# Row sums of an attention softmax: the inversion moved from VectorE's reciprocal to a power of minus one on GpSimd

## Chip, cores and metric

The kernel runs on one core of a Trainium2 chip. The metric is the device time of one execution in microseconds; lower is better. Below, PE is TensorE, DVE is VectorE, ACT is ScalarE, POOL is GpSimd and SP is SyncE, as in the profile.

## What is computed

Eight images of 256 channels and 32x32 points (1024 tokens) pass through three layers: a group norm with full softmax attention over 8 heads of 32 channels, a linear attention with rotary angles and a short convolution, and a feed-forward layer on a Haar transform. Only the first one's softmax is touched:

```python
weight = jnp.einsum('bct,bcs->bts', q * scale, k * scale)
weight = jax.nn.softmax(weight.astype(jnp.float32), axis=1)
a = jnp.einsum('bts,bcs->bct', weight, v)
```

The kernel keeps the axis s on the partitions and t, over which the softmax runs, along the free dimension, so that maximum and sum are taken within a partition.

## The kernel before

**Units and blocks.** One image has 64 units (`UNITS`): 2 groups of 4 heads (`NG`, `HG`), 8 blocks of 128 key positions (`NB`), and within a block the 4 heads of the group. Unit s makes one 128x1024 tile of scores: PE's `scores` (L653, two matmuls into one of two PSUM tiles ps_s), DVE's `maximum` (L1053, negmax), ACT's `exponentials` (L914), which writes probs and adds the rows up into `sums`. A PSUM tile comes free for the scores two units on when its exponential is done.

**Values.** When the 4 units of a block are through, its 128x4 sums are inverted, and the block's 128x128 values are multiplied by them (`v_scaled`, two buffers), which does the softmax's division on the smaller side. PE's `weigh_values` (L668, 16 matmuls) then adds probs times v_scaled into ps_o. Three steps on three engines, joined by semaphores: DVE's `invert_sums` (L1059) waits for probs_ready and raises rsums_ready; POOL's `scale_values` (L1330) waits for v_done, for pv_done (its buffer has been read), and for rsums_ready, and raises v_scaled_ready, for which `weigh_values` waits. There are 128 such blocks in all, 16 an image.

**Order.** Each engine runs its own instruction stream in order. The loops go over images in kinds (first, six steady, last, and an epilogue) and over the 64 units; behind a unit's own instruction stand the steps that tables such as `DVE_STEADY` or `POOL_STEADY` give to that slot. While image i is in its attention, the later layers of image i - 1 and the preparation of image i + 1 are spread over the same slots. In `DVE_STEADY`, `"invert"` has 16 slots (2, 5, 8, 12, ...), and in `POOL_STEADY`, `"scale"` has 16 (0, 5, 6, 12, 17, 17, 25, ...). Entries of one slot come in the order of the table.

**What else POOL does.** The square-root inverses of the norms (`rsqrt`: an addition L1361, ln_var, then a power with the exponent -0.5, L1364, ln_rs, with a wait of POOL on its own semaphore between), the convolution's products and sums (`lepe`: L1369, L1386, L1389), the mean of the keys (L1401, L1404, kmean), and the rotation of the queries (`turn_q`: L507, L511, L514). PE's denominators (L768) wait for kmean; PE's linear attention output (L781, "out") waits for the last L514 of its half of the heads, and DVE's L1199 follows it. PE's L741 projects queries and keys of the second layer, L749 transposes its keys. DVE's L1224 is the last addition of an image.

Of the kernel before, what the change touches and what calls it, by code (L numbers as in the profile page):

```python
# [13 lines left out]
P = 128  # L14
# [13 lines left out]

CONSTS = {}
_at = 0  # L30
for _name, _width in (("gn_mean", P), ("minus_half", 4), ("eps", 2), ("ident", P), ("head_mask", P),
                      ("head_mean", HG), ("pair_rows", P // 2), ("interp", NC * LL),
                      ("cos_tok", NB * D), ("sin_tok", NB * D),
                      ("cos_ch", L), ("sin_ch", L)):
    CONSTS[_name] = (_at, _at + _width)
    _at += _width
# [7 lines left out]
for _name, _width in (("bq", 2), ("bk", 2), ("bproj", 2), ("bqk", 4), ("lepe_w", 6), ("lepe_bias", 6),  # L44
# [19 lines left out]
    "copy": (36, 37), "pk0": (48, 56), "apply": (40, 43), "pq1": (12, 12), "pq0": (43, 44), "pk1": (20, 22),  # L64
}
DVE_FIRST = {
    "invert": (5, 9, 13, 17, 21, 25, 29, 33, 37, 41, 45, 49, 52, 57, 60), "w1": (25, 29), "pv0": (47, 62),
    "pk1": (21, 23), "pq1": (13, 13), "stats": (31, 32, 37, 38), "moments": (38,), "gn": (38,), "pq0": (45, 45),
    "pk0": (53, 57), "pv1": (2, 9),
}  # L70
# [18 lines left out]
DVE_STEADY = {  # L89
    "pv0": (47, 63), "norm1": (11, 14, 16, 16), "norm2": (42, 45, 46, 47), "pk1": (21, 21), "proj": (5, 7, 8, 9),  # L90
    "x1T": (10, 11, 12, 15), "kT": (24, 27, 31, 32), "kv": (30, 35),
    "invert": (2, 5, 8, 12, 16, 20, 25, 28, 32, 36, 41, 44, 48, 54, 56, 60), "denT": (33,),
# [21 lines left out]
    "qk": (18, 18, 21, 22, 24, 25, 28, 30),  # L114
}
DVE_LAST = {
# [126 lines left out]
def build(nc, x, wqkv_t, wproj_t, wqk, fc1_t, fc2_t, params, consts, out):  # L243
    with ExitStack() as ctx:
# [801 lines left out]
        def _(dve):  # L1046
# [6 lines left out]
                dve.tensor_reduce(negmax[:, s % 4:s % 4 + 1], ps_s[s % 2][:, :], AX_X, ALU.max, negate=True)\  # L1053
                   .then_inc(max_ready, 1)

            def invert_sums(i, g, j):
                n = NB * g + j
                dve.wait_ge(probs_ready, UNITS * i + HG * (n + 1))
                dve.reciprocal(rsums[:, j % 2, :], sums[:, j % 2, :]).then_inc(rsums_ready, 1)  # L1059

            def gn_statistics(b, n):

                c, half = n // 2, n % 2
# [190 lines left out]
            def step(kind, i, tile):  # L1254
                name, n = tile
                b = i - 1
                if name == "invert":
                    n = 2 * NB * i + n - (0 if kind == "first" else 1)
                    invert_sums(n // (2 * NB), n // NB % NG, n % NB)
                elif name == "w1":  # L1260
                    dve.wait_ge(made["w1"], n + 1)
                    dve.tensor_copy(w1[:, n * HALF:n * HALF + HALF], bank(tile)[:, :]).then_inc(weights_ready, 1)
                elif name == "norm1":
                    ln_normalise(b, n, x1_tokens(n), ln1_rsqrt, ln1_done)
                elif name == "norm2":
                    ln_normalise(b, n, t2_tokens(n), ln2_rsqrt, ln2_done)
                elif name == "add":
                    add_norm(dve, b, n)
                elif name == "lepe":
                    lepe_tail(b, n)  # L1270
                elif name == "late_turn":
                    turn_q(dve, b, n + 4)
                elif name == "stats":
                    gn_statistics(i + 1, n)
                elif name == "moments":
                    gn_moments(i + 1)
                elif name == "gn":
                    gn_group(i + 1)
                elif tile in SPLIT:
                    low_part(i, tile)  # L1280
                elif name in ("pv0", "pv1"):
                    values(i, tile)
                else:
                    post_tile(i, tile)
# [23 lines left out]
                        step(kind, i, tile)  # L1308

            def epilogue():  # L1310
                invert_sums(B - 1, NG - 1, NB - 1)
                for s in range(UNITS):
                    for tile in due("DVE", "epilogue", s):
                        step("epilogue", B, tile)
# [5 lines left out]
        def _(pool):  # L1320
            def scale_values(i, g, j):

                n = 2 * NB * i + NB * g + j
                pool.wait_ge(v_done, 4 * i + 2 * g + 2)
                if j >= 2 or not (isinstance(i, int) and i == 0 and g == 0):

                    pool.wait_ge(pv_done, 2 * (n - 1))
                pool.wait_ge(rsums_ready, n + 1)
                r = rsums[:, j % 2, :].rearrange("p (h o) -> p h o", o=1)
                pool.tensor_tensor(v_scaled[:, j % 2, :].rearrange("p (h d) -> p h d", h=HG),  # L1330
                                   v_tok[g][:, j, :].rearrange("p (h d) -> p h d", h=HG),
                                   r.to_broadcast([P, HG, D]), ALU.mult).then_inc(v_scaled_ready, 1)
# [125 lines left out]
def constants():  # L1458
# [15 lines left out]
    interp[np.arange(C), i0 + 1] = w  # L1474
    con["interp"][:] = interp.reshape(NC, P, LL).transpose(1, 0, 2).reshape(P, NC * LL)
    con["minus_half"][:] = -0.5
    con["eps"][:] = 1e-5
    inv_freq = (1.0 / np.float32(10000.0) ** (np.arange(0, D, 2, dtype=np.float32) / np.float32(D))).astype(np.float32)
    freqs = np.outer(np.arange(L, dtype=np.float32), inv_freq).astype(np.float32)
# [51 lines left out]
```

## Time and profile before

| | before |
|---|---|
| median of 3 runs | 1364.84 us (1364.63 to 1365.78) |
| the profiled execution | 1364.11 us |
| its span, first to last instruction | 1362.3 us |
| PE busy | 1235.3 us (91%) |
| DVE busy | 995.1 us (73%) |
| ACT busy | 879.5 us (65%) |
| POOL busy | 467.4 us (34%) |
| mean granted TensorE clock | 0.976 of 2.4 GHz |

Busy shares are averages over the whole span. A matmul counts as busy while it is in the pipeline, so 91% doesn't mean that PE is at its peak. The chain that ended last is found by going back from the last instruction, each time to what released it or to the instruction before it on its engine. "issue" is time in which the profile shows nothing that was waited for; where an instruction waits for two semaphores, the one that it names can be the wrong one.

### The profile page before, as it was taken

To read this page: it belongs to the slowest core of one execution; us is meant where nothing else is said; L and a number is where in the kernel's file an instruction comes from. 1 tells how busy PE (TensorE), PEld (TensorE's weight loads), DVE (VectorE), ACT (ScalarE), POOL (GpSimd) and SP (SyncE) were. 2 spreads that over 40 slices of the span, in tenths; PEclk is the share of its full clock that TensorE was granted. 3 is DMA by queue.
4 is the path that set the end of the run, shared out by engine and by line. 5 is a ranking of instruction groups with operands and counts; after the bars stand their busy time and mean duration, and the time that the engine had idled before them with its cause. 6 is when DMAs were issued, how large, how long until landed. Compare 5 with 4: busy or idle time off the path is not lost.

```text
span 1362.3 us, 22187 instructions
## 1 busy us (share of the span) xinstructions
PE 1235.3 (91%) x7972; PEld 644.5 (47%) x7972; DVE 995.1 (73%) x1609; ACT 879.5 (65%) x1457; POOL 467.4 (34%) x621
## 2 busy tenths in 40 slices
PE   6888899899998999899998999989998999979796
PEld 5544444544445454445444444454544444444373
DVE  3666687857889487866888578884879678884663
ACT  1666667675776668676775767766685767757422
POOL 2001017520285015630185203840166301850351
PEclk9998999999999999999999999999999999999897
DMA  8242415123442236223351234422262234300210
GB/s 275 58 108 45 106 40 134 34 63 101 110 112 47 52 109 139 48 63 93 92 116 27 66 117 101 105 57 58 88 140 48 62 93 110 80 15 0 80 33 31
DMA packets 51180, 110.84 MB, mean 81 GB/s; under 512 B 15456, under 2 KB 15840, under 8 KB 50816
## 3 DMA queue, kind: packets, MB, share of 16 engines
q1 hardware_dynamic: 48400, 100.39, 30.3%
q0 software_dynamic: 2480, 8.78, 2.3%
q8 instruction: 64, 1.05, 0.3%
q14 instruction: 44, 0.36, 0.1%
q10 hardware_dynamic: 192, 0.26, 0.1%
HBM read 21.81 MB, written 8.39 MB: 22 GB/s over the span
## 4 chain that ended last, share of the span: by engine, by line
PE 54%; DVE 29%; ACT 7%; issue 4%; POOL 2%; DMA 2%; SPq 1%; DVEq 0%; ACTq 0%; POOLq 0%
DVE negmax L1053 15%; PE ps_s L653 13%; PE ps_o L668 7%; PE work L741 6%; ACT probs L914 5%; PE work L680 4%; PE work L800 4%; PE work L727 4%; PE work L692 3%; DVE tok L1129 3%; DVE ln_st L1118 3%; PE work L805 3%; PE work L781 2%; DVE lo L1098 1%; PE work L715 1%
## 5 line engine op out<-in xcount | busy, mean ns | idle before, releaser
L914 ACT ACTIVATE probs<-ps_s,negmax 128x1024 f32<-128x1024 f32 x512 | 571.0, 1115 | 328.0 <-DVE negmax L1053 323.3
L1053 DVE TENSOR_REDUCE negmax<-ps_s 128x1 f32<-128x1024 f32 x512 | 618.8, 1216 | 220.0 <-PE ps_s L653 218.2
L653 PE MATMUL ps_s<-q_st,k_st 128*128 128x512 f32 x1024 | 407.8, 482 | 54.7 <-ACT probs L914 42.7
L653 PEld LDWEIGHTS ps_s<-q_st,k_st 128*128 128x128 f32 x1024 | 165.1, 192 | 294.4 <-ACT probs L914 163.3
L1330 POOL TENSOR_TENSOR v_scaled<-v_tok,rsums 128x128 f32<-128x128 f32 x128 | 56.0, 438 | 580.3 <-DVE rsums L1059 580.3
L668 PE MATMUL ps_o<-probs,v_scaled 128*32 128x512 f32 x2048 | 249.9, 606 | 1.3 <-POOL v_scaled L1330 1.3
L680 PE MATMUL work<-xg,w_qkv 128*128 128x512 f32 x256 | 120.7, 597 | 2.7 <-ACT xg L927 2.7
L741 PE MATMUL work<-ln_ch,w_qk 128*128 128x512 f32 x240 | 115.0, 601 | 3.6 <-DVE k_ch L1236 3.6
L668 PEld LDWEIGHTS ps_o<-probs,v_scaled 128*32 128x32 f32 x2048 | 53.9, 110 | 129.9 <-issue 117.7
L1389 POOL TENSOR_TENSOR x<-x,csum 128x1024 f32<-128x1024 f32 x45 | 107.5, 2389 | 2.5
L914 ACT ACTIVATION_READ_ACCUMULATOR probs<-ps_s,negmax 128x1 f32 x512 | 99.6, 195 | 0.0
L1361 POOL TENSOR_TENSOR ln_var<-ln_mv,con 128x2 f32<-128x2 f32 x64 | 12.9, 202 | 184.4 <-DVE ln_mv L1123 184.4
L800 PE MATMUL work<-band,w 128*128 128x512 f32 x120 | 63.6, 666 | 7.8 <-ACT band L996 6.0
L680 PEld LDWEIGHTS work<-xg,w_qkv 128*128 128x128 f32 x256 | 46.6, 189 | 44.2 <-issue 38.3
L692 PEld LDWEIGHTS work<-w_qkv,xg 128*128 128x128 f32 x512 | 63.6, 196 | 4.1 <-DVE lo L1098 1.4
L692 PE MATMUL work<-w_qkv,xg 128*128 128x128 f32 x512 | 64.0, 280 | 0.0
L741 PEld LDWEIGHTS work<-ln_ch,w_qk 128*128 128x128 f32 x240 | 43.0, 188 | 42.7 <-issue 29.8
L727 PE MATMUL work<-att,w_proj 128*128 128x512 f32 x120 | 56.8, 597 | 0.0
L1386 POOL TENSOR_SCALAR csum<-ln_ch,par 128x1024 f32<-128x1024 f32 x45 | 54.9, 1221 | 0.0
L805 PE MATMUL work<-shared,w 128*128 128x512 f32 x112 | 52.6, 592 | 0.0
L999 ACT ACTIVATE shared<-work,par 128x512 f32<-128x512 f32 x60 | 41.0, 689 | 16.2 <-PE work L800 16.1
L988 ACT ACTIVATE t<-work,par_elu 128x512 f32<-128x512 f32 x60 | 41.2, 687 | 10.9 <-PE work L741 10.9
(157 smaller groups left out, 1448.5 us busy)
## 6 DMA issues: line engine op xcount, KB each, us to landing
q_st<-hi SPq DMA_DIRECT2D x128, 128.0 KB, 2.4
q_st<-lo SPq DMA_DIRECT2D x120, 128.0 KB, 2.4
k_st<-t SPq DMA_DIRECT2D x224, 64.0 KB, 2.0
k_st<-hi SPq DMA_DIRECT2D x128, 64.0 KB, 2.8
k_st<-lo SPq DMA_DIRECT2D x128, 64.0 KB, 3.2
x<-in_x SPq DMA_DIRECT2D x8, 1024.0 KB, 6.1
out_x<-ln_ch SPq DMA_DIRECT2D x16, 512.0 KB, 2.8
xg<-in_x POOLq DMA_DIRECT2D x7, 1024.0 KB, 8.6
```

The costliest lines, as they stand in the source:

```text
L653: mm = pe.matmul(ps_s[s % 2][:, half * HALF:half * HALF + HALF], k_st[:, h, j * P:j * P + P], q_st[g][:, h, half * HALF:half * HALF + HALF ...
L668: mm = pe.matmul(ps_o[D * h:D * h + D, cols], v_scaled[:, j % 2, D * h:D * h + D], probs[:, j % 2, h, cols], start=(j == 0), stop=(j == NB ...
L680: mm = pe.matmul(bank(tile)[:, :], w_qkv[:, c, col:col + P], xg[:, c, half * HALF:half * HALF + HALF], start=(c == 0), stop=(c == NC - 1))
L692: mm = pe.matmul(bank(tile)[:, P * n:P * n + P], xg[:, c, P * nb:P * nb + P], w_qkv[:, c, col:col + P], start=(c == 0), stop=(c == NC - 1))
L727: mm = pe.matmul(ps[:, :], w_proj[:, g, P * c:P * c + P], att[:, g, half * HALF:half * HALF + HALF], start=(g == 0), stop=(g == 1))
L741: mm = pe.matmul(ps[:, :], w_qk[:, c, col:col + P], ln_ch[:, c, 1 + half * HALF:1 + half * HALF + HALF], start=(c == 0), stop=(c == NC - 1))
L800: pe.matmul(ps[:, :], w1[:, P * n:P * n + P], band[:, :], start=True, stop=True)\
L805: mm = pe.matmul(ps[:, :], w2[:, k, :], hid[:, k, :], start=(k == 0), stop=(k == 7))
L914: act.activation(probs[:, j % 2, h, :], ps_s[s % 2][:, :], ACT.Exp, bias=negmax[:, s % 4:s % 4 + 1], accum_out=sums[:, j % 2, h:h + 1]).th ...
L1053: dve.tensor_reduce(negmax[:, s % 4:s % 4 + 1], ps_s[s % 2][:, :], AX_X, ALU.max, negate=True)\
L1330: pool.tensor_tensor(v_scaled[:, j % 2, :].rearrange("p (h d) -> p h d", h=HG), v_tok[g][:, j, :].rearrange("p (h d) -> p h d", h=HG), r.t ...
L1389: pool.tensor_tensor(x1[:, c, :], x1[:, c, :], lepe_product, ALU.add).then_inc(lepe_step, 1)
```

## The change

Each inversion leaves DVE's stream. POOL makes it itself, inside `scale_values`: it waits for the exponentials (probs_ready), raises the 128x4 sums to the power of a constant -1, and waits for that result on rsums_ready before it scales. The slots of "invert" go from the four DVE tables, and the call at the head of DVE's epilogue goes too. A new constant `minus_one`, 4 columns wide, stands in the table of constants, all tiles behind it shift by 16 bytes. The slots of "scale" stay as they are.

```diff
-for _name, _width in (("gn_mean", P), ("minus_half", 4), ("eps", 2), ("ident", P), ("head_mask", P),
+for _name, _width in (("gn_mean", P), ("minus_half", 4), ("minus_one", 4), ("eps", 2), ("ident", P), ("head_mask", P),
...
-            def invert_sums(i, g, j):
-                n = NB * g + j
-                dve.wait_ge(probs_ready, UNITS * i + HG * (n + 1))
-                dve.reciprocal(rsums[:, j % 2, :], sums[:, j % 2, :]).then_inc(rsums_ready, 1)
-
...
-                if name == "invert":
-                    n = 2 * NB * i + n - (0 if kind == "first" else 1)
-                    invert_sums(n // (2 * NB), n // NB % NG, n % NB)
-                elif name == "w1":
+                if name == "w1":
...
             def epilogue():
-                invert_sums(B - 1, NG - 1, NB - 1)
...
                     pool.wait_ge(pv_done, 2 * (n - 1))
+                pool.wait_ge(probs_ready, HG * (n + 1))
+                pool.tensor_tensor(rsums[:, j % 2, :], sums[:, j % 2, :], const("minus_one"), ALU.pow)\
+                    .then_inc(rsums_ready, 1)
                 pool.wait_ge(rsums_ready, n + 1)
...
+    con["minus_one"][:] = -1.0
```

## Rows read from the trace of the kernel before

**Rows 1.** The page, part 4: the chain that ended last, by engine.

```profile
PE 54%; DVE 29%; ACT 7%; issue 4%; POOL 2%; DMA 2%; SPq 1%; DVEq 0%; ACTq 0%; POOLq 0%
```

**Rows 2.** Groups of POOL instructions: line, out<-in, count | busy us, mean ns | idle before.

```profile
L1364 POOL TENSOR_TENSOR ln_rs<-ln_var,con 128x2 f32<-128x2 f32 x64 | 44.8, 700 | 5.0
...
L1361 POOL TENSOR_TENSOR ln_var<-ln_mv,con 128x2 f32<-128x2 f32 x64 | 12.9, 202 | 184.4 <-DVE ln_mv L1123 184.4
...
L1404 POOL TENSOR_TENSOR kmean<-con,ksum_g 128x4 f32<-128x4 f32 x16 | 2.8, 202 | 0.6
```

**Rows 3.** Groups of DVE instructions, the same columns.

```profile
L1059 DVE RECIPROCAL rsums<-sums 128x4 f32<-128x4 f32 x128 | 21.6, 168 | 4.7 <-ACT probs L914 4.7
```

**Rows 4.** Waits: who waited for whom, us in total, times, longest us.

```profile
POOL v_scaled L1330 <- DVE rsums L1059: 580.3, 83, 21.4
...
PEld ps_o L668 <- POOL v_scaled L1330: 11.3, 19, 1.9
```

**Rows 5.** The chain in order of time: start us, us, what.

```profile
353.94 0.06 DVE rsums L1059
...
368.35 1.85 PE ps_o L668 x16
...
418.84 0.07 issue
...
1268.97 5.07 DMA x<-in_x
```

**Rows 6.** Timeline, blocks 15 and 19: start us, us, instruction [idle before <- releaser].

```profile
367.13 0.40 POOL L1330 TENSOR_TENSOR v_scaled<-v_tok,rsums 128x128 f32<-128x128 f32 x1
...
368.28 0.16 PEld L668 LDWEIGHTS ps_o<-probs,v_scaled 128*32 128x32 f32 x8 [0.76 <-POOL v_scaled L1330]
...
371.09 0.19 ACT L914 ACTIVATION_READ_ACCUMULATOR probs<-ps_s,negmax 128x1 f32 x1
...
372.38 0.40 POOL L1330 TENSOR_TENSOR v_scaled<-v_tok,rsums 128x128 f32<-128x128 f32 x1 [4.86 <-DVE rsums L1059]
```

**Rows 7.** Timeline, the same columns, blocks 23 and 27.

```profile
386.84 0.40 POOL L1330 TENSOR_TENSOR v_scaled<-v_tok,rsums 128x128 f32<-128x128 f32 x1
...
387.73 0.16 PEld L668 LDWEIGHTS ps_o<-probs,v_scaled 128*32 128x32 f32 x8 [0.36 <-issue]
...
389.58 0.73 PE L653 MATMUL ps_s<-q_st,k_st 128*128 128x512 f32 x2
...
390.89 1.22 DVE L1053 TENSOR_REDUCE negmax<-ps_s 128x1 f32<-128x1024 f32 x1
...
397.33 0.41 POOL L1330 TENSOR_TENSOR v_scaled<-v_tok,rsums 128x128 f32<-128x128 f32 x1
...
398.38 0.16 PEld L668 LDWEIGHTS ps_o<-probs,v_scaled 128*32 128x32 f32 x8 [0.17 <-issue]
...
401.35 0.63 PE L749 MATMUL work<-con,k_ch 128*128 128x128 f32 x4 [0.38 <-DVE k_ch L1236]
...
402.12 1.07 PE L768 MATMUL work<-shared,kmean 128*32 128x512 f32 x8
```

**Rows 8.** Timeline, last rotation and what waits for it, second and fourth steady image.

```profile
410.08 2.36 POOL L514 TENSOR_TENSOR shared<-shared,att 128x1024 f32<-128x1024 f32 x1
...
412.54 1.13 PE L781 MATMUL work<-kv_c,shared 128*128 128x128 f32 x8 [0.67 <-issue]
...
724.24 2.36 POOL L514 TENSOR_TENSOR shared<-shared,att 128x1024 f32<-128x1024 f32 x1
...
728.90 1.05 PE L781 MATMUL work<-kv_c,shared 128*128 128x128 f32 x8
```

**Rows 9.** Timeline, the last image's block 43.

```profile
1221.49 0.45 POOL L1330 TENSOR_TENSOR v_scaled<-v_tok,rsums 128x128 f32<-128x128 f32 x1
...
1221.99 0.20 PEld L668 LDWEIGHTS ps_o<-probs,v_scaled 128*32 128x32 f32 x8 [0.87 <-POOL v_scaled L1330]
```

**Rows 10.** One line's instructions: count: duration ns min/median/max, first and last start us.

```profile
L1330 POOL TENSOR_TENSOR v_scaled<-v_tok,rsums x128: 390/400/1200, 44.1 to 1267.5; 128x128 f32<-128x128 f32 x128
```

More of the change, by code:

```diff
@@ L66 @@
 DVE_FIRST = {
-    "invert": (5, 9, 13, 17, 21, 25, 29, 33, 37, 41, 45, 49, 52, 57, 60), "w1": (25, 29), "pv0": (47, 62),
+    "w1": (25, 29), "pv0": (47, 62),
     "pk1": (21, 23), "pq1": (13, 13), "stats": (31, 32, 37, 38), "moments": (38,), "gn": (38,), "pq0": (45, 45),
@@ L91 @@
     "x1T": (10, 11, 12, 15), "kT": (24, 27, 31, 32), "kv": (30, 35),
-    "invert": (2, 5, 8, 12, 16, 20, 25, 28, 32, 36, 41, 44, 48, 54, 56, 60), "denT": (33,),
+    "denT": (33,),
     "out": (37, 37, 41, 41), "fc2": (59,), "uT": (39, 40, 42, 43), "late_up": (0, 5), "pv1": (3, 4),
```

3 rows, old and new, of the table DVE_LAST are left out of this document.

## Prediction

> **What bounds the kernel now.** I read the page's chain first: 54% of it PE, 29% DVE, 2% POOL [rows 1]. The work of the images hangs on a loop of scores (L653), row maximum (L1053) and exponential (L914), with the rest of the kernel placed between; what counts is which engine has no slack where the change touches it. So I read next the groups of POOL and DVE that the change touches [rows 2, 3], then the waits of POOL [rows 4], the chain in order of time for one image in the steady state (333 to 490 us) [rows 5], and last the instructions around each of that image's 16 blocks of values [rows 6, 7, 8]. The reader should see two things. POOL waited 83 times, 580.3 us in all, for the reciprocal [rows 4]; these blocks have time to spare. The other 45 scalings start with no idle time before them, since POOL is behind with the convolution (L1386, L1389) or the rotation (L507 to L514), and TensorE starts the matmuls of several of them within half a microsecond of the scaling's end.
>
> I number a block by the last unit of its four heads, from 3 to 63; one image has 16.
>
> **What is removed.** 128 reciprocals on VectorE, 21.6 us busy, 168 ns each [rows 3]. Their worth is smaller. Where a DVE-bound stretch holds one, the chain gives it 0.06 us (353.94), since the next instruction starts before it has ended; one more like it, of 0.08, is all that the steady image has [rows 5]. Seven images with two each: 7 x 2 x 0.07 = 1.0 us gained. The upper bound is 128 x 0.17 = 22 us, if each one stood on the path; the chain says otherwise.
>
> **What is added.** 128 powers on GpSimd, shape 128x4. Before has the power at 128x2 only: ln_rs, 64 times, 700 ns, beside 202 ns for an addition of the same shape [rows 2]. So two columns cost 0.50 us more than plain arithmetic. A multiplication of 128x4 (kmean, 202 ns a piece) [rows 2] costs what one of 128x2 does, so the base doesn't grow. If the 0.50 us is by column, 128x4 takes 0.20 + 2 x 0.50 = 1.20 us; if it is a fixed part, 0.70 us. These are my two ends. [...] The scaling that follows waits for the power; between ln_var and ln_rs, the same kind of hand-over, the chain has 0.07 us (418.84) [rows 5]. So a block costs POOL 1.27 us more (low end 0.77), 128 x 1.20 = 154 us of new work on an engine that is idle most of the time.
>
> The page "GPSIMD Engine Reference" of the Trainium skill (section "Performance versus the Vector engine") gives some 2.6 cycles an element for two-input arithmetic and puts the rest into the start of an instruction. Were that all there is, the two further columns would cost next to nothing, which speaks for the low end and would give the sum of the second rival below; but by that figure 128x2 and 128x2 as a power would cost the same, and the trace has 202 against 700 ns, so it doesn't describe a power.
>
> **What moves.** The wait for the exponentials goes from DVE's queue to POOL's. The reciprocal stood in DVE's order behind later maxima; the power can start some 0.16 us (an estimate, the size of the other hand-overs) after the block's last exponential. Block 19 is the tightest of those where POOL was idle: its exponential ended at 371.09 + 0.19 = 371.28, its scaling began at 372.38 [rows 6] and would now begin at 371.28 + 0.16 + 1.27 = 372.71, 0.33 us late, long before TensorE asks for it. In the others the reciprocal came so much later that a power of 1.20 us gives the values as early or earlier. Behind the wait in POOL's queue stand the same instructions as before, and they are let go earlier. No DMA and no other queue is passed; the loads of constants grow by 16 bytes a row.
>
> **What it costs where POOL is busy,** in the steady image, with 1.27 us a block; TensorE begins 0.05 us after a scaling that it truly waited for (1221.49 + 0.45 against 1221.99) [rows 9].
> - Block 15: scaling ended 367.53, weight load at 368.28 [rows 6]: cover 0.75 - 0.05 = 0.70. Wait 0.57 us. The chain holds this very matmul group (368.35, 1.85) [rows 5]: all 0.57 counts.
> - Block 23: POOL is 0.33 late from block 19, without idle since. 387.24 + 0.33 + 1.27 + 0.05 = 388.89 against 387.73: wait 1.16. The scores behind end at 390.31 and their maximum starts at 390.89 [rows 7], so 0.58 is hidden and 0.58 counts.
> - Block 27: POOL is late by 0.33 + 2 x 1.27 = 2.87: 397.74 + 2.87 + 0.05 = 400.66 against 398.38 + 0.58: wait 1.70. Behind it TensorE has 0.38 us idle before L749 and some 0.1 before the denominators (L768 at 402.12) [rows 7], of which I take 0.45 as cover: 1.25 counts.
> - Block 31: it stands in front of four long rotations. The last, L514, ends at 412.44, and TensorE starts L781 at 412.54 [rows 8], which the profile calls "issue", though it waits for that result. DVE's L1199 follows. Cover about 0.1 us: 1.17 counts.
> - The others: block 39 would make TensorE wait too, but its next scores are made a whole maximum ahead of their use; 35, 43 and 47 have more time between scaling and matmul than two powers take; in the first image POOL is idle for nearly all. Nothing.
>
> Together 0.57 + 0.58 + 1.25 + 1.17 = 3.57 us an image. The pattern of L514 and L781, 0.1 us apart, stands in five of the six steady images (one is shown) [rows 8]; in the fourth TensorE gets there late by itself (L514 ended at 726.60, L781 began at 728.90) [rows 8], so it pays 2.40. 5 x 3.57 + 2.40 = 20.3. The last image has POOL well ahead until block 43, where TensorE already waits (1221.99) [rows 9]: 1.27. The final block, also 1.1 us late, is covered by the residual's transfer, 5.07 us from 1268.97 [rows 5]; without that cover it would cost 1.1. Sum: 20.3 + 1.3 - 1.0 = 20.6 us. The profiled execution took 1364.11 us, of which 1362.3 are the span; the median of the runs is 1364.84, 0.7 above it. Forecast: 1364.84 + 20.6, about 1385 us.
>
> **The rivals.**
> - Power by a fixed cost, 0.70 us (0.77 a block). Block 15 costs 0.07, block 23 waits 0.16 and hides it, block 27 costs 0.3, block 31 0.67: 1.0 an image, 5.6 for six, 0.8 in the last, less 1.0: +5.4, 1370 us. For it: no other shape shows growth from two to four columns. Chance 0.22. In between (0.95 us, 1.02 a block) the same sum gives +12.5, 1377 us: 0.15.
> - Faster: DVE becomes the winner. By the chain it bounds two stretches of some 15 us in each image, with about six reciprocals in or beside them. If each is worth its full 0.17 us, that is 1.0 us an image, 7 us in all; it wins only if a power on 128x4 costs no more than about 0.45 us, less than the 128x2 does now. The loss is then some 2 us at block 31: 1360 us. Also needed: that the chain's 0.07 is an artefact. Chance 0.07.
> - The waits are taken up elsewhere, because DVE or ScalarE was as late as TensorE: 1362 to 1367 us. Against it: blocks 15 and 31 stand on the chain. Chance 0.06.
> - A lock between DVE and POOL. A scaling takes 400 ns, but at most 1200 [rows 10]; that is block 3's, which begins while DVE runs L1224. The power could meet such instructions too, up to 0.8 us each, 14 of them: +11 on top at most; but it comes some 2 us earlier than they do. It is inside the range's upper part. The page "SBUF — State Buffer" of the Trainium skill (section "Who interferes with whom") has this as an exclusive lock between GpSimd and a DVE instruction with two SBUF inputs, held for the whole instruction; the trace's 1200 against 400 ns agrees.
>
> **How the numbers follow.** Main case 0.50, 1381 to 1389 us. Range 1366.5 to 1389: it takes in the low and middle price of the power and leaves out the faster case, most of the "taken up" case and a power above 1.3 us. What the measurement can tell from no change is 0.2%, 2.7 us: slower means above 1367.6, faster below 1362.1. Faster 0.07; same 0.13 (the "taken up" case and the lower part of the fixed-cost one); slower 0.80.
>
> **What would show it.** The power's mean time, 1.2 or 0.7 us, settles the largest term. Waits of the ps_o matmuls for v_scaled should rise from 11.3 us (19 times) to some 25 us or more, at blocks 15, 23 and 27 of each steady image; the distance from L514 to L781 should stay 0.1 us, with both about a block's cost later; the first image should take as long as before. An image period that grows without these waits, or DVE stretches that shrink by more than 0.2 us an image, would prove me wrong.

## The result, and the profile after

The changed kernel takes 1382.85 us in the median (1381.65 to 1391.22), the kernel before 1365.31 on the same chip: 1.0141 times as long, with a 95% interval of 1.0116 to 1.0166. The forecast was 1385 us. Of the changed kernel the profiled execution took 1383.46 us, with a span of 1381.7; that of before had 1364.11 and 1362.3.

Busy time by engine, then the chain by engine (part 4 of the page), both of after; the chain of before is [rows 1]:

```profile
PE 1229.3 (89%) x7972; PEld 643.5 (47%) x7972; DVE 991.0 (72%) x1481; ACT 876.7 (63%) x1457; POOL 598.1 (43%) x749
...
PE 41%; DVE 26%; POOL 14%; ACT 9%; issue 7%; DMA 1%; SPq 1%; DVEq 0%; ACTq 0%; POOLq 0%
```

POOL's share of the chain went from 2% to 14%. The groups of the power and of the scaling behind it (line, out<-in, count | busy us, mean ns | idle before), and then the waits (who waited for whom: us, times, longest):

```profile
L1319 POOL TENSOR_TENSOR rsums<-sums,con 128x4 f32<-128x4 f32 x128 | 129.8, 1014 | 470.8 <-ACT probs L913 457.5 <-PE ps_o L667 13.3
...
L1323 POOL TENSOR_TENSOR v_scaled<-v_tok,rsums 128x128 f32<-128x128 f32 x128 | 56.2, 439 | 10.1
...
PEld ps_o L667 <- POOL v_scaled L1323: 27.7, 22, 2.5
...
PE ps_o L667 <- POOL v_scaled L1323: 16.6, 22, 1.6
```

A power of 128x4 takes 1.01 us (forecast 1.20; the low end was 0.70). The hand-over to the scaling is 0.08 us, the 10.1 us of idle time divided by 128. So a block costs POOL 1.09 us, not 1.27. TensorE's weight loads wait 27.7 us for scaled values, where [rows 4] had 11.3: the "25 us or more" of the forecast. A matmul and its load wait together, so the two lines are not added.

**Where the time went.** I put the same points of both traces, the landmarks, side by side, and took the time after minus that of before, in us. The columns are: the start of TensorE's `weigh_values` of block 3 and of block 15, the start of the denominators (L767 after, L768 before), the end of the last rotation, the start of the last of VectorE's L1193 (L1199 before) behind the group means, and `weigh_values` of blocks 47 and 63. The group means are TensorE's two small matmuls L697 (L698 before) for the next image's group norm. They stand between the last rotation and that last L1193.

| image | 3 | 15 | denominators | last rotation | L1193 | 47 | 63 |
|---|---|---|---|---|---|---|---|
| 1 | 1.90 | 2.25 | 2.89 | 3.97 | 2.36 | 2.15 | 2.10 |
| 2 | 2.09 | 2.39 | 3.03 | 4.13 | 5.72 | 6.36 | 6.26 |
| 3 | 6.26 | 6.57 | 6.49 | 7.59 | 9.19 | 9.06 | 9.00 |
| 4 | 8.99 | 9.28 | 9.91 | 11.04 | 10.08 | 10.70 | 10.64 |
| 5 | 10.64 | 10.94 | 11.55 | 12.64 | 12.65 | 13.28 | 13.23 |
| 6 | 13.22 | 13.51 | 14.12 | 15.22 | 16.81 | 17.41 | 17.67 |

Read image 5 across: -0.10 at block 11 (10.54, a landmark not in the table), +0.39 at block 15, +0.61 up to the denominators, +1.09 up to the last rotation, 0.01 up to L1193, +0.63 up to block 47, -0.05 up to block 63: 2.6 us. The 1.9 us ahead of image 1 are taken for chance: a second profile of the same kernel (below) has 0.00 there. From the other rows two things stand out that the forecast did not have: a step of 1.6 us, up or down, in front of L1193 in images 1, 2, 3 and 6; and 0.6 us ahead of block 47 in images 2, 4, 5 and 6, with a fall of 0.1 to 0.2 in 1 and 3. Beside these, image 4 gives back 1 us behind the rotation, which the forecast did have. The sum: 0.20 + 4.17 + 2.74 + 1.65 + 2.59 + 4.45 = 15.8 in the six images (column 63 minus column 3), 1.9 ahead of them, and 2.4 up to block 63 of the last image (20.04 there): 20.0 us. The spans differ by 19.4, so that the residual's transfer covered 0.6.

**The steps of the forecast, as rows.** Timeline of after, image 2, the stretches of blocks 15 and 27, and of the denominators (start us, us, instruction [idle before <- releaser]); before has [rows 6, 7]:

```profile
369.13 1.01 POOL L1319 TENSOR_TENSOR rsums<-sums,con 128x4 f32<-128x4 f32 x1
370.22 0.40 POOL L1323 TENSOR_TENSOR v_scaled<-v_tok,rsums 128x128 f32<-128x128 f32 x1
370.67 0.16 PEld L667 LDWEIGHTS ps_o<-probs,v_scaled 128*32 128x32 f32 x8 [1.16 <-POOL v_scaled L1323]
...
400.65 1.02 POOL L1319 TENSOR_TENSOR rsums<-sums,con 128x4 f32<-128x4 f32 x1
401.75 0.40 POOL L1323 TENSOR_TENSOR v_scaled<-v_tok,rsums 128x128 f32<-128x128 f32 x1
402.10 2.00 POOL L506 TENSOR_TENSOR att<-att,con 128x1024 f32<-128x1024 f32 x1
404.06 0.19 POOL L1394 TENSOR_TENSOR ksum_g<-ksum 128x2 f32<-128x2 f32 x1
...
402.20 1.92 PE L667 MATMUL ps_o<-probs,v_scaled 128*32 128x512 f32 x16 [1.37 <-POOL v_scaled L1323]
...
402.83 0.74 DVE L1230 SCALAR_TENSOR_TENSOR k_ch<-work,par_elu,t 128x512 f32<-128x512 f32 x1
...
405.15 1.07 PE L767 MATMUL work<-shared,kmean 128*32 128x512 f32 x8
```

At block 15 TensorE waits for a scaling that ends at 370.62, and starts 0.05 us later. At block 27 it has been waiting 1.37 us. But the last rows show what this wait is worth: the denominators need k_ch from DVE, and DVE isn't late by it. Its last L1230 starts 2.37 us after its counterpart, exactly as late as block 19 was (2.38). It ends at 403.57, and the sums' small copy (ksum_g) starts 0.49 us later, since POOL is still in the rotation L506; before, that distance was 0.15. L767 then starts 1.09 us behind ksum_g (before 0.77), since TensorE, late by block 27's matmuls, has scores and L748 to run first. These 0.34 + 0.32 us are what blocks 23 and 27 leave on the path.

### The profile page after: what moved, and what is told of

It reads as the page before. It is cut to its first block, busy times and chain, and to the rows that moved or that the text cites. A ratio compares the mean times of both kernels' runs of the same rounds, so it can differ in the third digit from the quotient of the medians.

```text
span 1381.7 us, 22187 instructions
## 1 busy us (share of the span) xinstructions
PE 1229.3 (89%) x7972; PEld 643.5 (47%) x7972; DVE 991.0 (72%) x1481; ACT 876.7 (63%) x1457; POOL 598.1 (43%) x749
## 3 DMA queue, kind: packets, MB, share of 16 engines
q8 instruction: 64, 1.05, 0.3%
## 4 chain that ended last, share of the span: by engine, by line
PE 41%; DVE 26%; POOL 14%; ACT 9%; issue 7%; DMA 1%; SPq 1%; DVEq 0%; ACTq 0%; POOLq 0%
DVE negmax L1052 13%; PE ps_s L652 10%; PE ps_o L667 7%; ACT probs L913 7%; POOL x L1382 6%; PE work L799 4%; PE work L726 4%; PE work L679 3%; PE work L691 3%; DVE tok L1123 3%; DVE ln_st L1112 3%; PE work L804 3%; POOL csum L1379 3%; PE work L780 2%; POOL rsums L1319 1%
## 5 line engine op out<-in xcount | busy, mean ns | idle before, releaser
L1319 POOL TENSOR_TENSOR rsums<-sums,con 128x4 f32<-128x4 f32 x128 | 129.8, 1014 | 470.8 <-ACT probs L913 457.5
L1323 POOL TENSOR_TENSOR v_scaled<-v_tok,rsums 128x128 f32<-128x128 f32 x128 | 56.2, 439 | 10.1
```

The lines of the kernel that those rows point to most:

```text
L1319: pool.tensor_tensor(rsums[:, j % 2, :], sums[:, j % 2, :], const("minus_one"), ALU.pow)\
```

## Experiments

**Theories.** A: the time comes from POOL's extra work, 1.09 us a block, at the few places where the path passes POOL. B: it comes from the hand-over and the moved wait, whatever the work in front of the scaling costs. C: two effects stand beside it, TensorE's clock behind a gap, and a lock at block 43, in which an instruction of VectorE is held up until one of POOL has ended.

**The changed kernel once more,** for the landmarks that hold from run to run.

> The changed kernel once more, as the measure for the others. Its profile had 4.2 us more than before in a steady image where the matmuls behind the gn_mom wait ran at half speed (images 2, 3 and 6), and 2.6 us where they did not differ from before (image 5). If that count holds, the pattern per block comes back to 0.1 us (block 15 +0.4, block 23 +0.45, last rotation +1.1, image's end +0.64) and the median is 1381 to 1384 us. If the 1.4 us that the profile lost in front of the first block were part of the change, they come back too; if they are chance, this run has another number there.

1382.07 us (1.0114, 1.0080 to 1.0148). The landmarks are those of the table: +0.38 us at block 15, +0.6 up to the denominators (not in image 3, as in the table), +1.09 at the rotation, +0.62 ahead of block 47 in images 2, 4, 5 and 6, -0.2 and -0.1 in 1 and 3. Block 3 of image 1 is on time (0.00), and block 63 of image 6 14.54 us late. The step of 1.6 us falls elsewhere: image 1 gives back 0.4 rather than 1.6, image 2 has none. That step varies between the two profiles; the rest doesn't.

**Both,** and **neither:** do the reciprocals or the powers make the time?

```diff
 # both (against after): VectorE inverts as before, GpSimd powers into a tile that nobody reads
+invert_sums, "invert" entries of the tables as before
-pool.tensor_tensor(rsums[:, j % 2, :], sums[:, j % 2, :], const("minus_one"), ALU.pow).then_inc(rsums_ready, 1)
+pool.tensor_tensor(unused[:, j % 2, :], sums[:, j % 2, :], const("minus_one"), ALU.pow).then_inc(rsums_pool, 1)
+pool.wait_ge(rsums_pool, n + 1)
 # neither (against before): no reciprocal, no power
-pool.wait_ge(rsums_ready, n + 1)
-r = rsums[:, j % 2, :].rearrange("p (h o) -> p h o", o=1)
+pool.wait_ge(probs_ready, HG * (n + 1))
+r = const("minus_one").rearrange("p (h o) -> p h o", o=1)
```

> The power is added on GpSimd at the same place, its result unused, and VectorE's reciprocals stay and are used. This is the addition alone. Theory (POOL's time in front of blocks 15 to 47 and of the last rotation is what costs): as slow as the changed kernel or slower by the worth of the reciprocals, 0 to 2 us, so 1382 to 1386 us. Rival (the reciprocals' removal gave back much, 0.17 us each where VectorE bounds, about 7 us, and hid a larger cost): 1388 to 1391 us.

> The inversion is left out on both engines (the values are scaled by minus one instead of by the inverted sums; this is the part of the computation that is missing); POOL waits for the exponentials directly. This is the removal alone. Theory: the reciprocals stood on the chain twice an image with 0.06 to 0.08 us, so 1 to 2 us faster than before, 1363 to 1364.5 us. Rival (VectorE is the winner of the change): 7 us faster, about 1358 us.

The kernel called neither leaves the inversion out of the computation. Against 1367.13 us of before: both 1385.39 (1.0131, 1.0099 to 1.0164), neither 1364.85 (0.9971, 0.9948 to 0.9994). Both is 3.3 us over the changed kernel's second run, neither 2.3 under before: two differences of the size of the scatter, which agree all the same that the reciprocals are worth 2 to 3 us in all. The landmarks of both say where: the 0.1 us at block 11 isn't gained, and the step up to block 23 is 0.2 us longer, 0.3 us an image. The forecast had 0.14.

**Widths:** the price of a power by its shape. In front of the kernel before, GpSimd runs power, multiplication and power again at each of eight widths, each one waiting for the last.

```diff
+for w in (1, 2, 3, 4, 8, 16, 32, 64):
+    for op in (ALU.pow, ALU.mult, ALU.pow):
+        pool.wait_ge(probe_done, done)
+        pool.tensor_tensor(csum[:, 2, 0:w], csum[:, 0, 0:w], csum[:, 1, 0:w], op).then_inc(probe_done, 1)
```

> The kernel before with 24 extra GpSimd instructions at its very start: powers and multiplications over 1, 2, 3, 4, 8, 16, 32 and 64 columns, one behind the other. Power at 2 columns was 0.70 us and at 4 columns 1.01 us. Theory (a fixed 0.38 us and 0.157 us for each column): 1 column 0.54, 3 columns 0.85, 8 columns 1.64, 64 columns 10.4 us. Rival (steps of four columns or a cost that flattens): 3 columns as 4, and 8 columns well under 1.6 us. Multiplications: 0.20 us at 1 to 8 columns, 0.3 at 64.

Groups of widths, two powers and one multiplication in each:

```profile
L1444 POOL TENSOR_TENSOR csum<-csum 128x64 f32<-128x64 f32 x3 | 21.4, 7138 | 0.2
...
L1444 POOL TENSOR_TENSOR csum<-csum 128x8 f32<-128x8 f32 x3 | 3.5, 1175 | 0.2
L1444 POOL TENSOR_TENSOR csum<-csum 128x4 f32<-128x4 f32 x3 | 2.2, 739 | 0.2
L1444 POOL TENSOR_TENSOR csum<-csum 128x3 f32<-128x3 f32 x3 | 1.9, 633 | 0.2
L1444 POOL TENSOR_TENSOR csum<-csum 128x2 f32<-128x2 f32 x3 | 1.6, 534 | 0.2
L1444 POOL TENSOR_TENSOR csum<-csum 128x1 f32<-128x1 f32 x3 | 1.3, 438 | 0.2
```

With the 0.20 us of a multiplication taken out (the shortest of these instructions took 0.19), a power takes 0.56 us at one column, 0.70 at two, 0.85 at three, 1.01 at four and 1.66 at eight, and 10.55 at 64 (the longest one). That is 0.39 us + 0.156 a column. Both of my ends were wrong in form: there is a fixed part of 0.2 us over plain arithmetic, and the rest is by column. The whole kernel took 1412.42 us in its one run; what it takes beyond before is about the length of these 24 instructions.

**One block's inversion back on VectorE,** for block 31, 27 or 43 of each image. ON_DVE is (7,), (6,) or (10,); the other blocks are as after. VectorE's `invert_sums` and its table entries are back, and it returns at once for the blocks that aren't in ON_DVE.

```diff
+if n % (2 * NB) in ON_DVE:
+    pool.wait_ge(rsums_ready, sum(m % (2 * NB) in ON_DVE for m in range(n + 1)))
+else:
     pool.wait_ge(probs_ready, HG * (n + 1))
     pool.tensor_tensor(rsums[:, j % 2, :], sums[:, j % 2, :], const("minus_one"), ALU.pow)\
-        .then_inc(rsums_ready, 1)
-pool.wait_ge(rsums_ready, n + 1)
+        .then_inc(rsums_pool, 1)
+    pool.wait_ge(rsums_pool, sum(m % (2 * NB) not in ON_DVE for m in range(n + 1)))
```

> The changed kernel, but block 31 of each image is inverted by VectorE's reciprocal in its old place; the other 15 by the power. Theory of the forecast (its fourth bullet): POOL's four rotations in front of L781 lose only this power, so the distance from the denominators to the last rotation's end goes back by 1.09 us in each image and five images get 1.1 us shorter: 5.5 us less than the changed kernel, 1376 to 1377 us. Rival (the rotations are late because of blocks 23 and 27 too): the distance from the denominators stays as it was, under 1 us less in all.

Block 31 alone on VectorE gives 1369.03 us (before 1366.29; 1.0037, 1.0014 to 1.0060). Block 63 of image 6 is 4.27 us later than in before, where the changed kernel's second run has 14.54: one of an image's sixteen powers gives back 10.3 us, twice what I expected. From the denominators to the last rotation the images lose 0.02 us, not 1.09: 6 x 1.06 = 6.4 us less than in that second run. Another 6.2 us less lie one step later, up to L1193, in images 1, 3, 4 and 6 (1.3, 1.6, 1.7, 1.6); those of image 4 are a stall of TensorE that this profile doesn't have (see "The gap"). (Together this is more than 10.3, since this profile begins image 1 1.7 us later.) Timeline of this kernel, image 2, to be set beside the rows of after under "The gap":

```profile
411.79 2.38 POOL L516 TENSOR_TENSOR shared<-shared,att 128x1024 f32<-128x1024 f32 x1
...
414.27 1.13 PE L783 MATMUL work<-kv_c,shared 128*128 128x128 f32 x8 [0.55 <-issue]
...
421.92 0.35 PE L700 MATMUL work<-gn_mom,con 128*128 128x4 f32 x2 [1.46 <-POOL gn_mom L1348]
422.14 0.71 PE L655 MATMUL ps_s<-q_st,k_st 128*128 128x512 f32 x2
422.69 1.06 PE L783 MATMUL work<-kv_c,shared 128*128 128x128 f32 x8
```

TensorE stands idle 1.46 us in front of the group means, and the matmuls behind run at their usual 0.71 us. In front of L783 it stands idle 0.55 us, where after has 1.68 in front of the same matmuls (L780): this one power makes both gaps longer.

> The changed kernel, but block 27 of each image is inverted by VectorE. The forecast's third bullet had 1.25 us an image for it: 7 us less in six images, 1375 us. The changed kernel's trace says that TensorE's wait at block 27 (+0.97 us) is mostly gone again at the denominators (+0.2 us behind block 23): then 1 to 2 us less in all, 1380 to 1381 us. In both cases the wait for v_scaled at block 27 should vanish.

Block 27 on VectorE: 1382.04 us (1.0108, 1.0072 to 1.0144), the median of the changed kernel. The 0.6 us an image that the landmarks give, 3.6 in all, are within that interval, which is 5 us to either side; the medians neither show nor exclude them. The landmarks are finer. TensorE's wait at block 27 is gone (-0.13 us at block 27 against block 23, where the changed kernel has +0.96), and yet the denominators come only 0.6 us earlier than in the changed kernel's second run, counted from block 23: now they are as late as block 19 was (-0.43 and -0.42 in image 2). So of the 0.43 and 0.96 us by which TensorE starts later at blocks 23 and 27, the first costs nothing and the second 0.6. POOL:

```profile
398.20 2.00 POOL L509 TENSOR_TENSOR att<-att,con 128x1024 f32<-128x1024 f32 x1
400.92 0.19 POOL L1411 TENSOR_TENSOR ksum_g<-ksum 128x2 f32<-128x2 f32 x1 [0.73 <-DVE k_ch L1240]
```

Here POOL waits for k_ch, where after had the two lines back to back.

> The changed kernel, but block 43 of each image is inverted by VectorE. The forecast had it at nothing in the six steady images and at 1.3 in the last. Theory from the changed kernel's trace: its power pushes POOL's first L519 against VectorE's normalisation (L1123), which then takes 1.41 us for the pair in place of 0.73, and each image ends 0.64 us later. Without this power the pair is back at 0.73 us, 6 x 0.64 + 1.0 = 4.9 us less, 1377 us. Rival (the longer pair is hidden by the maxima, and the 0.64 us come from elsewhere): the pair is short again but only the last image's 1.0 us comes back.

Block 43 on VectorE: 1378.72 us (1.0093, 1.0062 to 1.0124). First after, then this kernel, image 2, POOL and DVE:

```profile
437.16 1.01 POOL L1319 TENSOR_TENSOR rsums<-sums,con 128x4 f32<-128x4 f32 x1
438.25 0.40 POOL L1323 TENSOR_TENSOR v_scaled<-v_tok,rsums 128x128 f32<-128x128 f32 x1
438.60 1.28 POOL L519 TENSOR_TENSOR t<-t,tok 128x512 f32<-128x512 f32 x1
...
438.94 1.41 DVE L1123 TENSOR_SCALAR tok<-t,ln_mv,ln_rs 128x256 f32<-128x256 f32 x2
```

```profile
435.56 0.40 POOL L1340 TENSOR_TENSOR v_scaled<-v_tok,rsums 128x128 f32<-128x128 f32 x1 [0.30 <-DVE rsums L1063]
435.92 1.28 POOL L522 TENSOR_TENSOR t<-t,tok 128x512 f32<-128x512 f32 x1
...
437.08 0.73 DVE L1133 TENSOR_SCALAR tok<-t,ln_mv,ln_rs 128x256 f32<-128x256 f32 x2
```

After has the pair of normalisations beginning 0.34 us behind the start of POOL's addition t<-t,tok, and it takes 1.41 us (so in all six images): the first of the two takes 1.09 us and ends 0.15 us behind POOL's addition, the second takes its usual 0.40. Without the power in front, POOL's addition has 0.12 us left when the pair starts, and the pair takes 0.73, as it does in all six images of before. The two read and write SBUF only. The maximum that follows comes 0.68 us later, POOL's next addition waits 0.55 us for VectorE's result, and in this kernel blocks 43 and 47 lie 0.62 us closer than in the second run in images 3 to 6. The median is 3.4 us under that of the second run, 6 x 0.62 = 3.7. This is the lock that the forecast had as a rival, at a place that it did not look at. The page "SBUF — State Buffer" of the Trainium skill (section "Who interferes with whom") gives the ports that POOL and VectorE share to whichever instruction was issued first, until it ends, and names tensor_scalar among those of VectorE that can ask for them; 1.41 against 0.73 us, with POOL first, agrees. What I did not try is to move the addition alone, without the power.

**Multiplication in place of the power,** by the same constant, which leaves the inversion out: what does the place cost, without the price?

```diff
-pool.tensor_tensor(rsums[:, j % 2, :], sums[:, j % 2, :], const("minus_one"), ALU.pow)\
+pool.tensor_tensor(rsums[:, j % 2, :], sums[:, j % 2, :], const("minus_one"), ALU.mult)\
```

> The changed kernel with a multiplication by minus one in place of the power: same instruction count, waits and hand-overs, but 0.20 us instead of 1.01 (the inversion is the part left out). Theory (time of POOL in front of blocks counts, not the hand-over): block 31 costs 0.27 us in place of 1.09, blocks 15 and 23 nothing since 0.27 is under their cover of 0.45 to 0.7, the pair of L1123 stays short or nearly, the gap before the group means is about 1.5 us: 0 to 2 us slower than before. Rival (the wait moved to POOL and the second semaphore cost): more than 5 us slower.

1368.42 us (1.0016, 1.0001 to 1.0031). Its group shows 203 ns. Blocks 15, 23 and 27 and the denominators are not late at all, the last rotation is 0.28 us late in each image (0.20 + 0.08 for the hand-over), block 43 has no lock (the pair takes 0.73). Theory B falls: with the same waits in the same places, 1.09 us a block cost 15 to 17.5 us, 0.28 cost 2.5.

**Warm:** eight matmuls of a constant in front of the group means, in the changed kernel (first), and in the kernel before. This uses the kernel's own keep_warm of two matmuls, four times; the profile shows two instructions for each of them, 16 in all.

```diff
-    "x1T": (9, 9, 10, 13), "gn": (39,), "pk0": (51, 53),
+    "x1T": (9, 9, 10, 13), "warm": (39, 39, 39, 39, ), "gn": (39,), "pk0": (51, 53),
```

> The changed kernel with eight matmuls of 128x128 on constants put into TensorE's idle time in front of the group means (L697) of each steady image, about 1 us of work in a gap of 2.1 us. Theory: TensorE's matmuls run at half speed for some 3.4 us behind this gap in images 2, 3, 5 and 6 (two matmuls of scores 1.20 us in place of 0.71), at 1.6 us lost each; with the gap filled the step between the group means and the last L1193 is 0.0 us in all images, and the kernel is 4 to 6 us faster than the changed one, 1376 to 1378 us. Rival (the half-speed stretches come by the throttle's own time, not by the gap): they stand in as many images as before, and the time is that of the changed kernel.

> The kernel before with the same eight matmuls in front of the group means of each steady image. Its gap there is 1.6 us and half-speed matmuls followed it in images 1 and 5. Theory: both stretches go, 3 us faster than before (ratio 0.998), none elsewhere. Rival (a gap of 1.6 us does nothing by itself, the stretches are chance): same time as before within 0.1%.

**The gap.** This is what the step of 1.6 us is made of. Timeline of after, image 2, TensorE, and then of warm (the changed kernel with these matmuls):

```profile
424.32 0.36 PE L697 MATMUL work<-gn_mom,con 128*128 128x4 f32 x2 [2.07 <-POOL gn_mom L1331]
424.54 0.71 PE L652 MATMUL ps_s<-q_st,k_st 128*128 128x512 f32 x2
425.08 1.80 PE L780 MATMUL work<-kv_c,shared 128*128 128x128 f32 x8
426.54 1.20 PE L652 MATMUL ps_s<-q_st,k_st 128*128 128x512 f32 x2
427.54 1.56 PE L780 MATMUL work<-kv_c,shared 128*128 128x128 f32 x8
```

```profile
420.23 1.95 PE L866 MATMUL work<-con 128*128 128x128 f32 x16
422.46 0.36 PE L697 MATMUL work<-gn_mom,con 128*128 128x4 f32 x2 [0.28 <-POOL gn_mom L1331]
422.67 0.71 PE L652 MATMUL ps_s<-q_st,k_st 128*128 128x512 f32 x2
423.22 1.05 PE L780 MATMUL work<-kv_c,shared 128*128 128x128 f32 x8
424.03 0.71 PE L652 MATMUL ps_s<-q_st,k_st 128*128 128x512 f32 x2
```

Eight matmuls of L780 take 1.80 us behind a gap of 2.07 us, and 1.05 behind one of 0.28. The granted clock of after in this stretch (start:end and length in us, then busy us of PE, PEld, DVE, ACT and POOL with their instructions, PEclk, DMA share, GB/s):

```profile
416.00:424.00 8.00, 5.52 (x38) 3.27 (x38) 6.86 (x16) 3.92 (x9) 3.02 (x7) 1.00 0.02 3
424.00:429.00 5.00, 4.68 (x23) 4.43 (x24) 3.26 (x9) 2.43 (x5) 3.08 (x11) 0.66 0.00 0
429.00:435.00 6.00, 5.52 (x33) 2.45 (x32) 5.71 (x12) 3.89 (x5) 2.67 (x5) 1.00 0.00 0
```

A mean of 0.66 over five microseconds is a mixture of the two levels, 2.4 and 1.2 GHz. I took the length of this gap and the mean clock of the 4 us behind it from all fourteen profiles, six images each:

| gap in front of the group means | kernels | images | clock below 0.75 behind it |
|---|---|---|---|
| 2.06 to 2.08 us | after, again, both, 27, 43 | 25 | 18 |
| 1.57 to 2.05 | before, busy, neither, multiplication, widths | 25 | 7 |
| 1.43 to 1.47 | image 4 of these ten; block 31 on VectorE | 16 | 2 |
| 0 to 0.29 | the three with the eight matmuls | 18 | 0 |

In the pair of the first table, before has the low clock here in images 1 and 5, after in 2, 3, 5 and 6: the steps of 1.6 us. The kernels of the first row also have 1.6 to 1.8 us of idle time in front of L780, about 8 us earlier, where before has 0.7. It doesn't suffice by itself: warm has 1.65 us there and no low clock in its first five images. What the profiles don't separate is which of the two longer gaps raises the share from 7 of 25 to 18 of 25.

The same happens at other places. In image 4 TensorE stops inside the 128 matmuls of L757, for which the profile shows no cause:

```profile
722.20 0.27 PE L757 MATMUL work<-tok,shared 128*32 128x32 f32 x8 [1.79 <-issue]
722.40 1.63 PE L653 MATMUL ps_s<-q_st,k_st 128*128 128x512 f32 x4
723.96 3.09 PE L668 MATMUL ps_o<-probs,v_scaled 128*32 128x512 f32 x16
```

These are rows of before, where the clock is 0.62 from 722 to 726 us and 16 matmuls for ps_o take 3.09 us rather than 1.92. The stall and the low clock are why TensorE comes late to L781 there [rows 8]. After has the same in its image 4: 2.00 us, 0.57 in the 4 us behind, 2.46 for the 16 matmuls. Eleven profiles have this stall in one image. Behind the seven of 1.74 to 2.07 us the clock is low, behind the three of 1.12 to 1.67 (both, 43, multiplication) it isn't, and it isn't behind one of 2.25 (warm, image 6). Block 31 on VectorE and the other two kernels with the eight matmuls have no such stall.

Some 6 to 11 us behind block 43, where the matmuls of L800 start, before has it in images 1, 2, 3 and 5 (0.50 to 0.62 in the lowest 3 us), after in 2 and 5 only. That is the 0.8 us that images 1 and 3 gained against before in that stretch, and with it the delay ahead of block 47 is the same 0.6 in all six.

The changed kernel with the eight matmuls takes 1376.99 us (1.0086, 1.0058 to 1.0114), 5.1 less than its second run. The kernel before with them takes 1361.74 us (beside 1365.89 of before; 0.9966, 0.9947 to 0.9984), and its landmarks lie 1.6 us earlier behind the group means in images 1 and 5. They also lie 2.9 us earlier in image 4, where the stall ahead of these matmuls is missing, so not all that they gain is shown to come from the filled gap. With the gap filled on both sides the change still costs 1.2% (1.0086 / 0.9966 = 1.0120, where the two runs of the changed kernel have 1.0141 and 1.0114). So the low clock costs both kernels. What it adds to the difference between them is 0.9 us by these medians, and 3.5 us by the table (an estimate: five images, 1.6 us, 18 of 25 less 7 of 25); the intervals of some 3 us on each ratio don't decide between the two. Which image of one kernel gets the low clock is not settled: the same gap had it in one image and not in the next, and it changed between two profiles of one kernel.

**Powers where POOL has time,** reciprocals at blocks 15 to 47 as before; then the same with the eight matmuls.

```diff
+ON_DVE = (3, 4, 5, 6, 7, 8, 9, 10, 11)
```

> The power only for the seven blocks of an image at which POOL is idle (3, 7, 11, 51, 55, 59, 63); blocks 15 to 47 keep VectorE's reciprocal. Theory: no wait for v_scaled at blocks 15, 23, 27, no longer pair of L1129, no late rotation, and the two reciprocals of 0.07 us taken off the chain: 0 to 1.5 us faster than before (ratio 0.999 to 1.000). Rival (a power costs something wherever it stands, by the hand-over or the port): over 2 us slower.

> Both together: the power for the seven blocks with an idle POOL, the reciprocal for the others, and the eight matmuls in front of the group means. If the two effects add: 3 to 4 us faster than before (ratio 0.997 to 0.998).

Busy takes 1364.96 us (0.9992, 0.9972 to 1.0011), no difference from before. 56 powers, 0.06 to 0.10 us gained at block 11 in each image, and nothing lost at any landmark: in the idle parts the power is free, and the reciprocal it replaces nearly so. With the matmuls, 1362.23 us (0.9964, 0.9949 to 0.9979), the same as those matmuls alone: no version is faster than the kernel before with them.

| kernel | us, median | ratio to before, 95% |
|---|---|---|
| after | 1382.85 | 1.0141, 1.0116 to 1.0166 |
| after, again | 1382.07 | 1.0114, 1.0080 to 1.0148 |
| both | 1385.39 | 1.0131, 1.0099 to 1.0164 |
| neither | 1364.85 | 0.9971, 0.9948 to 0.9994 |
| after, 31 on VectorE | 1369.03 | 1.0037, 1.0014 to 1.0060 |
| after, 27 on VectorE | 1382.04 | 1.0108, 1.0072 to 1.0144 |
| after, 43 on VectorE | 1378.72 | 1.0093, 1.0062 to 1.0124 |
| after, multiplication | 1368.42 | 1.0016, 1.0001 to 1.0031 |
| after, eight matmuls | 1376.99 | 1.0086, 1.0058 to 1.0114 |
| before, eight matmuls | 1361.74 | 0.9966, 0.9947 to 0.9984 |
| powers where POOL has time | 1364.96 | 0.9992, 0.9972 to 1.0011 |
| the same, eight matmuls | 1362.23 | 0.9964, 0.9949 to 0.9979 |

## Why the prediction was right, and where it was not

The direction and the size were right: 1382.85 us against 1385, slower by 17.5 us against 20.2. The mechanism was too: POOL's queue at a few blocks, little gained on VectorE. But that the sum came out within 2.2 us is in part luck: three terms that were too large (the power, block 23, block 27) and two that were missing cancel. Point by point:

- **The power, 1.20 us.** It measured 1.01. The step that failed is "if the 0.50 us is by column", which rested on one shape: of the 0.50 that separates a power from plain arithmetic at two columns, 0.19 is fixed and 0.31 is by column. What GpSimd does inside a power, no run shows; only these times. The in-between rival had 0.95 for it and 1377 us; the whole kernel lies further from that than from the forecast, for the reasons below. (What the prediction calls the second rival, beside the 2.6 cycles, is the first of its list, the fixed cost.)
- **The reciprocals, 1.0 us gained.** The landmarks give 0.15 us an image as they stand (0.08 up to block 11, 0.07 behind block 47; the forecast had 0.14), and 0.3 when they stand in the kernel beside the powers; the medians give 2 to 3 us for all. The order was right: 21.6 us of busy time are worth no more than 3. The rival in which VectorE wins falls twice, by the price of the power and by this.
- **Block 15, 0.57.** It measured 0.40, and with the measured price the step is exact: 1.09 - 0.70 = 0.39.
- **Block 23, 0.58.** TensorE did come 0.45 us later, but it cost nothing: with block 27's power gone, the denominators are as late as block 19 was. The step that failed is to take the scores and the maximum behind this block for the path; the denominators wait for the last L1230, and that was not late by it.
- **Block 27, 1.25.** It cost 0.6. TensorE waited 1.37 us; the cover of 0.45 that I took was TensorE's own idle time, and the true one was larger, since TensorE itself would soon have waited for VectorE. Half of what was left came by POOL: ksum_g starts 0.49 us behind k_ch, where before had 0.15. The other 0.3 us are TensorE's own queue behind block 27's matmuls.
- **Block 31, 1.17.** It measured 1.09 (0.28 in the kernel with the multiplication, 0.02 with the inversion back on VectorE). Right in place and mechanism, the 0.1 us from the last rotation to L781 stands, and the fourth image gives 1.0 of it back, as forecast. But TensorE is late there by a stall and the low clock behind it, in before and in after. In the three kernels that have a shorter stall and the full clock behind it, image 4 gives back 2.2 to 2.5 us, so that the 1.0 hangs on what both profiles happened to have. Block 31 was the largest measured term, and taking this one power off POOL gives back over two thirds of the loss (1.0037 against 1.0114), a part of it through the clock and the missing stall.
- **The others, "nothing".** Wrong at block 43. My reason was that there is more time between scaling and matmul than two powers take, and for TensorE it is so. But the power also moves the instruction behind the scaling, POOL's addition, by 0.75 us against block 43's matmuls, and there it meets a pair of VectorE: 0.6 us an image. I had the lock as a rival, and asked only whether the power itself would meet such an instruction; it didn't, 997 to 1188 ns. The scaling met one, at block 63 rather than block 3 (1.35 us in five images), at no cost.
- **TensorE's clock.** Missing. The forecast treated every microsecond of TensorE as equal; it stood at one granted clock, and never asked how long TensorE stood idle ahead of it. The gap in front of the group means grew from 1.6 to 2.07 us, and the low clock behind it costs 1.6 us each time: +1.6 in images 2, 3 and 6, -1.6 in image 1, 0 in image 5, where both kernels have it. Less twice 0.8 behind block 43, this is 1.6 us in this pair of profiles. Over more runs the eight matmuls take 5.1 us from the changed kernel and 4.2 from before, and the table's counts give 3.5 us for the change: its share of the 17.5 us stays open between about 1 and 4.
- **The last image, 1.27.** Block 43 measured 1.08, and 1.3 more came up to block 63. Of this the residual's transfer covered 0.6 (the forecast had 1.1 there, all covered).

With measured terms a steady image sums to 0.40 + 0.6 + 1.09 + 0.62 less 0.15 = 2.6 us, against the forecast's 3.57 less 0.14. Six of them, less 1.0 in image 4 and 0.7 in image 3 (its denominators, for which POOL was 0.86 us behind k_ch in before already), are 13.9; the clock adds 1.6 and the last image 2.4, less 0.6 under the transfer: 17.3, and 1.9 by chance ahead of image 1 make 19.2 of the 19.4 between the spans. The forecast had 20.6. The range was made by the price of the power, and it held.

## What to carry to other kernels

- Before you move an operation to an idle engine, look not at the share of time that it is idle, but at each place where it isn't. Here taking the power away from one block in sixteen, the one in front of the rotations, gave back about two thirds of the loss, and 56 powers in idle places cost nothing.
- A wait of TensorE in the profile is no cost until you have asked what it would have waited for next. Blocks 23 and 27 came 1.4 us later between them and cost 0.6. Look for the landmark behind, not for the wait.
- An instruction that grows also moves the ones behind it in its queue: check these for what they then run beside, and check the gaps that other engines then have.

## What the hardware showed that I had not expected

- A power on GpSimd takes about 0.39 us + 0.156 a column of 128 partitions, from 1 to 64 columns (0.56 to 10.55 us), where a multiplication takes 0.20 at up to 8 columns and 0.32 at 64.
- VectorE's normalisation (a tensor_scalar with two scalars by partition, SBUF to SBUF, 128x256) is held up by an addition of 128x512 that POOL began before it: 1.41 us a pair against 0.73, in every image. The held-up instruction has one input tile only, where the scaling's 1200 ns [rows 10] stood beside one of VectorE with two (L1224).
- A gap of 2.07 us in TensorE's work was followed by a stretch at 1.2 GHz, which costs 1.6 us here, in 18 of 25 images, one of about 1.6 to 2.0 in 7 of 25, one of 1.45 in 2 of 16, and a filled one in none of 18. So a gap that grows by 0.4 us can cost 1.6 more in an image. With eight small matmuls of a constant in the gap the kernel before is 0.34% faster, part of which may be image 4's missing stall.
